# Layer 0's finish: gate in 64-row tiles on half of two banks, x reloaded in 2 KB runs, gate, z and transposes on every fourth token

## The chip, the cores and the metric

The kernel runs on one core of a Trainium2 chip. The number that counts is the device time of one execution in microseconds (us). The profile is one execution taken by the hardware profiler; its times are microseconds from the span's start unless marked ns. PE is TensorE's matmul side, PEld its weight loads, DVE is VectorE, ACT is ScalarE, POOL is GpSimd, SP is the engine that issues the DMAs.

## What is computed

The input x is 256 x 256 positions ("tokens") of 64 channels. Two layers follow each other. Layer 0, which the change touches, is

```
g  = group_norm(x)                      # 32 groups of 2 channels over all tokens
zn = layer_norm(g) * w + b              # over the 64 channels of a token
a  = sigmoid(zn @ w_ag + b_ag) * (zn @ w_ap + b_ap);  b = the same with w_bg, w_bp
p[i,j,c] = sum_k a[i,k,c] * b[j,k,c]    # 64 products of 256 x 256 matrices
x  = x + (layer_norm(p) @ w_z + b_z) * sigmoid(zn @ w_g + b_g)
```

Layer 1 has the same shape, with norms over the whole tensor. Its input is the x of the last line above, group-normalised.

## The kernel before

Rows of x (256 tokens each) are handled in groups of four: 64 groups, NG = 64, GR = 4. Two tokens share a column of the data kept on chip: partitions 0 to 63 hold the channels of an even token, 64 to 127 those of the odd token beside it, so a group is a 128 x 512 tile, four blocks of 128 token pairs. XT_ALL holds zn, transposed in this manner, as a high and a low half in fp16; `half(g, 0)` and `half(g, 1)` are those of group g, each 512 columns in token order. w_hi and w_lo (in EFF) are the two fp16 halves of the weights. The gate's weights stand there as a 128 x 128 matrix with two 64 x 64 blocks on the diagonal (one for the even, one for the odd token) and zeros beside them.

Layer 0 goes through these stages, in time: x is loaded and transposed (L515), normalised, split into halves; then four chunks of channels, each with a projection (L501 with EFF,XT_ALL, in units of eight rows) and an einsum (L501 with AB); the products p go to DRAM (p_scratch). In the projection every second unit is computed in 64-row tiles: two matmuls on partitions 0 to 63 and 64 to 127 with 64 columns each, writing two banks. The other units use 128-row matmuls with 128 columns. Both take x as the loaded operand ("weights" in the profile's sense) and the layer's weights as the streamed one.

Then comes layer 0's finish, the stage of the change, 64 groups in one software pipeline. On TensorE, step k does, in this order:

- 4 transposes of the scaled p of group k (L782), from tile pn into bank 4 or 5;
- the gate of group k (`project_gate`, 12 matmuls of 128 x 128), into bank 0 or 1 in turn, after a wait for the sigmoid of group k-2 (`sg_done`). Groups 0 to 3 (AHEAD = 4) were done before, in banks 0 to 3, in the last chunk;
- z of group k-1: a bias matmul of 512 columns (PS<-BROW,ONES) and 4 fp32 matmuls with pt as loaded operand and w_out streamed (PS<-EFF,WK; the trace shows each as two records), into bank 6 or 7;
- 4 transposes of the new x of group k-3 (L814), from tile xb, into bank 2 or 3.

ACT evicts the transposed p into pt (L993), applies the sigmoid to the gate (L998) and writes the high half of the new x (L1006). DVE scales half of p (L1427), multiplies z by the gate (L1436), writes the low half of the new x (L1450) and takes its statistics (L1442); at steps 3, 6 and 9 it also computes a further quarter of the layer norm's factors (reciprocal L1372 and what follows). POOL scales the other half of p (L1058) and adds the gated z to x (L1067). SP loads p (L415) and x (L421) ahead, x in 16 rows per slot (xb, four slots, two DMAs each), as `x_tok`: for a row of x, partition p takes tokens 2p and 2p+1, 512 bytes in a run. The engines are ordered by semaphores alone; the code's order is the order on each engine.

After the finish comes layer 1: its projection and einsum in four chunks, and its own finish, whose transposes (L767) read a tile at every fourth column, `x1sum[:, g%4, r:BANK:GR]`. The stage that loads x at the start of the kernel already uses `x_runs`, in which partition 32r + p takes eight tokens of row r, 2 KB in a run.

Of the kernel before, what the change touches and what calls it, by code (L numbers as in the profile page):

```python
# [34 lines left out]
CH = 64  # L35
P = 128
# [56 lines left out]
def build(nc, x, mask, w0, w1, bias0, bias1, vecs, consts, norm_consts, spread, ones3, out):  # L93
# [7 lines left out]

    x_tok = x[0].rearrange("r (p q) c -> p r (q c)", q=2)
    x_runs = x[0].rearrange("(g r) (p w) c -> (r p) g (w c)", r=GR, w=2 * GR)
# [6 lines left out]
    with ctx:  # L110
# [82 lines left out]
        ptb = AB[:, 0:2 * CH * BR * 2].rearrange("p (s m n) -> p s m n", s=2, n=2 * BR)  # L193
        xb = AB[:, 2 * CH * BR * 2:4 * CH * BR * 2].rearrange("p (s r m) -> p s r m", s=HS, m=ROW)

# [157 lines left out]
        def mask_tile(eng, n4, u):  # L353
# [3 lines left out]
                                     rows.unsqueeze(2).to_broadcast([P, 2, 2 * CHUNK, PR]), ALU.mult)  # L357

        def reached(eng, semaphore, value):

            if not isinstance(value, int) or value > 0:
                eng.wait_ge(semaphore, value)
# [3 lines left out]
        def _(sp):  # L366
# [22 lines left out]
            for layer in range(2):  # L389
# [29 lines left out]
                def load_rows(row, s):  # L419
                    for h in range(2):  # L420
                        sp.dma_start(xb[:, s, h * HR // 2:(h + 1) * HR // 2, :],  # L421
                                     x_tok[:, ds(row + h * HR // 2, HR // 2), :]).then_inc(xb_in[s], 16)

# [48 lines left out]
                load_rows(0, 0)  # L472
                load_rows(HR, 1)
                load_p(BR, 1)
                load_rows(2 * HR, 2)
                load_rows(3 * HR, 3)

                with sp.Fori(0, NB // 2 - 1) as b2:
                    for s in range(2):
                        for h in range(2):  # L480
                            slot = 2 * s + h
                            row = sp.snap(b2 * (2 * BR) + (slot * HR + HS * HR))
                            p_row = sp.snap(b2 * (2 * BR) + (s * BR + 2 * BR))
                            groups = sp.snap(b2 * (2 * BG) + ((slot + 1) * HG))
                            tiles = sp.snap(b2 * (2 * BG) + ((s + 1) * BG))

                            sp.wait_ge(x1tr_done, groups)
                            load_rows(row, slot)
                            if h == 0:

                                sp.wait_ge(tb_done, tiles)
                                load_p(p_row, s)
# [6 lines left out]
        def _(pe):  # L499
# [116 lines left out]
            for layer in range(2):  # L616

                free = sqp_ready if layer == 0 else st_ready

                def rows_times(bank, g, r, column):  # L620

                    dst = bank[:, r * ROW:(r + 1) * ROW]
                    hi, lo = (half(g, i)[:, r * P:(r + 1) * P] for i in range(2))
                    mm(dst, hi, w_hi[:, ds(column, ROW)], True, False)
                    mm(dst, hi, w_lo[:, ds(column, ROW)], False, False)
                    return mm(dst, lo, w_hi[:, ds(column, ROW)], False, True)

# [40 lines left out]
                def project_gate(g):  # L668
                    if layer == 0:
                        for r in range(GR):  # L670
                            last = rows_times(PS[:, g if g < AHEAD else g % 2, :], g, r, E_G)
                        last.then_inc(g_done, 1)
                    else:
                        bank, hi, lo = PS[:, g % 4, :], w_hi[:, E_G:E_Z], w_lo[:, E_G:E_Z]
                        mm(bank, hi, half(g, 0), True, False)
                        mm(bank, lo, half(g, 0), False, False)
                        mm(bank, hi, half(g, 1), False, True).then_inc(gate1_done, 1)
# [97 lines left out]
                for step in range(NG + 3):  # L775
# [8 lines left out]
                    if AHEAD <= g < NG:  # L784

                        pe.wait_ge(sg_done, g - 1)
                        project_gate(g)
                    g = step - 1
                    if 0 <= g < NG:

                        pe.wait_ge(pt_ready, g + 1)
                        reached(pe, y_done, g - 1)
                        bank = PS[:, 6 + g % 2, :]
                        mm(bank, ONES3[:, :], BROW[:, :].unsqueeze(1).to_broadcast([P, GR, ROW]), True, False)
                        for r in range(GR):
                            last = mm(bank[:, r * P:(r + 1) * P], pt[:, g % 2, r * P:(r + 1) * P], w_out,
                                      False, r == GR - 1)
                        last.then_inc(z_done, 1)
                    g = step - 3
                    if 0 <= g < NG:  # L800

                        pe.wait_ge(xadd_done, g + 1)
                        if g < 2:

                            pe.wait_ge(sg_done, g + 3)
                        if g < NG - 2:

                            reached(pe, x1split_done, g - 1)
                        else:

                            pe.wait_ge(sg_done, NG)
                        for r in range(GR):
                            row = g * GR + r
                            last = nc.tensor.transpose(PS[:, new_x_bank(g), r * P:(r + 1) * P],  # L814
                                                       xb[:, row // HR % HS, row % HR, :], ident)
                        last.then_inc(x1tr_done, 1)
# [13 lines left out]
        def _(act):  # L830
# [54 lines left out]
            for layer in range(2):  # L885
# [99 lines left out]
                def finish_steps(g0, n_steps, lo):  # L985

                    for k in range(n_steps):
                        g = g0 + k
                        if lo[0] <= k < lo[1]:
# [7 lines left out]
                            reached(act, xadd_done, g - 3)  # L997
                            nc.scalar.activation(sg[k % 4], PS[:, k if ahead else k % 2, :], ACT.Sigmoid,  # L998
                                                 scale=T[:, 22:23]).then_inc(sg_done, 1)
                        if lo[2] <= k < lo[3]:  # L1000
                            h = g - 4

                            act.wait_ge(x1tr_done, h + 1)
                            act.wait_ge(bn_done, h + (1 + NG))
                            bank = new_x_bank(h) if isinstance(h, int) else 2 + k % 2
                            nc.scalar.activation(half(h, 0), PS[:, bank, :], ACT.Identity, scale=T[:, 25:26]  # L1006
                                                 ).then_inc(x1t_ready, 1)
# [11 lines left out]
        def _(pool):  # L1019
# [22 lines left out]
            def finish_steps(g0, n_steps, lo):  # L1042
                for k in range(n_steps):
# [16 lines left out]
                    if lo[2] <= k < lo[3]:  # L1060
# [4 lines left out]
                        pool.wait_ge(y_done, h + 1)  # L1065
                        rows = xb[:, slot, u * GR:(u + 1) * GR, :].rearrange("p r m -> p (r m)")
                        nc.gpsimd.tensor_tensor(rows, rows, sg[(k + 1) % 4], ALU.add).then_inc(xadd_done, 1)  # L1067
# [39 lines left out]
        def _(dve):  # L1107
# [14 lines left out]
            def col(i):  # L1122
                return T[:, i:i + 1]
# [191 lines left out]
            for layer in range(2):  # L1315
# [128 lines left out]
                def split(k, g, lo):  # L1444

                    if lo[6] <= k < lo[7]:
                        h = g - 5
                        dve.wait_ge(x1t_ready, h + 1)
                        bank = new_x_bank(h) if isinstance(h, int) else 2 + (k + 1) % 2
                        V.scalar_tensor_tensor(half(h, 1), PS[:, bank, :], col(25), half(h, 0),  # L1450
                                               ALU.mult, ALU.subtract).then_inc(x1split_done, 1)
# [139 lines left out]
```

## Time and profile before

| | |
|---|---|
| median of 3 runs | 1089.46 us (1088.4 to 1090.19) |
| profiled execution | 1086.74 us, its span 1084.9 us |
| granted TensorE clock over the span | 0.964 |
| TensorE matmul busy | 982.9 us, 91% of the span |
| DVE, ACT, POOL busy | 774.3, 677.2, 558.3 us |
| layer 0's finish | from 487.5 to about 659 us |

The span is the time from the first to the last instruction of the program that was profiled. In the trace a matmul's record starts when it enters the array and ends after its modelled latency, so records overlap; the pace of matmuls is read from the distance of their starts, and a merged row "start, length, x12" says where twelve of them began. A busy share of 100% on PE says that no gap was seen between such overlapping records.

### The profile page before, as it was taken

Reading aid. Unit: us, or ns where it says so; the run is one execution under the profiler, and the core shown is the slowest. Engines: PE = TensorE matmul, PEld = TensorE weight load, DVE = VectorE, ACT = ScalarE, POOL = GpSimd, SP = SyncE. Lnnn points to the kernel's source line nnn. Section 1 sums busy time; section 2 is a strip of 40 time slices with the busy share of each in tenths; the row PEclk is TensorE's granted clock in tenths of the full one; section 3 lists DMA queues with packets and bytes.
Section 4 is the critical chain, followed back from the end, with each engine's and each line's share of the span. In section 5 each row is a group of like instructions: output and inputs, shape, how many; then the busy total and the mean of one; then the engine's idle time right before and its main releaser. Section 6 shows DMA issues by size and latency. Waiting matters only on the chain.

```text
span 1084.9 us, 38124 instructions
## 1 busy us (share of the span) xinstructions
PE 982.9 (91%) x15292; PEld 783.0 (72%) x15292; DVE 774.3 (71%) x1278; ACT 677.2 (62%) x1098; POOL 558.3 (51%) x480
## 2 busy tenths in 40 slices
PE   5688888699999999969999995899999999799997
PEld 5533333498888988968999994778878787655554
DVE  6926777876868868678888887655646565567776
ACT  5747666555656666555777674676858676546665
POOL 0002555783470916506777772572918457146664
PEclk9979999799999999989999997899999999889999
DMA  9900000002203021279998930004040220699994
GB/s 342 350 10 1 2 2 2 2 4 78 81 6 153 4 98 61 59 212 255 210 199 185 209 74 1 3 13 147 4 139 22 75 86 11 179 214 272 286 282 156
DMA packets 173205, 121.80 MB, mean 112 GB/s; under 512 B 69764, under 2 KB 152068, under 8 KB 173064
## 3 DMA queue, kind: packets, MB, share of 16 engines
q1 hardware_dynamic: 173064, 119.67, 41.2%
q8 instruction: 119, 1.95, 0.8%
q14 instruction: 22, 0.18, 0.1%
HBM read 69.32 MB, written 50.33 MB: 110 GB/s over the span
## 4 chain that ended last, share of the span: by engine, by line
PE 80%; DVE 7%; DMA 4%; ACT 3%; POOL 2%; issue 2%; SPq 1%; DVEq 0%; POOLq 0%; ACTq 0%
PE PS L501 70%; DMA AB<-x 3%; PE PS L767 3%; PE PS L782 3%; PE PS L814 2%; PE PS L588 2%; POOL XT_ALL L1023 1%; POOL AB L356 1%; PE PS L515 1%; DMA AB<-k_scratch 1%; DVE XT_ALL L1450 1%; ACT XT_ALL L866 1%; ACT WK L903 1%; SPq L370 1%; DVE XT_ALL L1290 0%
## 5 line engine op out<-in xcount | busy, mean ns | idle before, releaser
L501 PE MATMUL PS<-EFF,XT_ALL 64*128 64x64 f16 (+1 forms) x10368 | 344.5, 201 | 11.0 <-POOL XT_ALL L1023 3.4
L501 PEld LDWEIGHTS PS<-EFF,XT_ALL 64*128 64x128 f16 (+1 forms) x10368 | 317.3, 97 | 44.3 <-issue 18.6
L501 PE MATMUL PS<-AB 64*128 64x128 bf16 (+2 forms) x2058 | 233.5, 282 | 12.3 <-POOL AB L1087 6.2
L903 ACT ACTIVATE WK<-PS,T 128x512 f32<-128x512 f32 x256 | 174.5, 685 | 95.5 <-PE PS L501 85.1
L501 PEld LDWEIGHTS PS<-AB 64*128 64x128 bf16 (+2 forms) x2058 | 197.3, 121 | 48.1 <-issue 13.1
L1087 POOL TENSOR_TENSOR AB<-WK,AB 128x512 f32 x128 | 145.1, 1161 | 111.4 <-ACT AB L913 110.6
L356 POOL TENSOR_TENSOR AB<-WK,MS 128x512 f32 x96 | 130.5, 1387 | 104.9 <-DVE WK L1323 104.9
L1023 POOL TENSOR_TENSOR XT_ALL<-AB,XT_ALL 128x512 f16<-128x512 f32 x60 | 71.1, 1189 | 144.0 <-DVE XT_ALL L1290 137.6
L1097 POOL TENSOR_TENSOR WK<-XT_ALL 128x512 f32 (+1 forms) x64 | 81.9, 1282 | 76.3 <-PE PS L767 50.9
L1331 DVE TENSOR_TENSOR WK<-PS,WK 128x512 f32<-128x512 f32 x128 | 85.8, 686 | 33.3 <-ACT WK L903 33.1
L1323 DVE TENSOR_TENSOR WK<-PS,WK 128x512 f32<-128x512 f32 x128 | 86.8, 689 | 29.1 <-ACT WK L903 23.5
L1347 DVE BATCH_NORM_STATS2 REC<-WK 128x512 f32 x64 | 44.4, 694 | 56.8 <-ACT WK L932 56.8
L954 ACT ACTIVATE WK<-PS,T 128x512 f32<-128x512 f32 x64 | 49.4, 777 | 51.4 <-PE PS L501 51.4
L932 ACT ACTIVATE WK<-PS,T 128x512 f32<-128x512 f32 x64 | 44.0, 687 | 51.7 <-PE PS L501 51.7
L501 PE MATMUL PS<-XT_ALL,AB 128*128 128x512 f32 x128 | 74.2, 669 | 0.0
L939 ACT ACTIVATE WK<-PS 128x512 f32<-128x512 f32 x64 | 41.2, 644 | 47.3 <-PE PS L501 45.6
L866 ACT ACTIVATE XT_ALL<-PS,T,CF 128x512 f32<-128x512 f32 x64 | 49.7, 776 | 33.1 <-PE PS L501 32.6
L501 PE MATMUL PS<-AB,EFF 128*128 128x512 f32 x128 | 67.4, 613 | 2.2 <-DMA AB<-k_scratch 2.2
L501 PEld LDWEIGHTS PS<-EFF,WK 128*128 128x128 f32 x512 | 68.1, 194 | 1.8
L1058 POOL TENSOR_TENSOR WK<-AB,S 128x256 f32<-128x256 f32 x64 | 50.5, 789 | 36.2 <-DVE S L1375 35.7
L501 PE MATMUL PS<-EFF,WK 128*128 128x128 f32 x512 | 68.3, 277 | 0.0
L993 ACT ACTIVATE WK<-PS 128x512 f32<-128x512 f32 x64 | 38.2, 597 | 47.4 <-PE PS L782 47.4
(193 smaller groups left out, 1541.4 us busy)
## 6 DMA issues: line engine op xcount, KB each, us to landing
AB<-x SPq DMA_DIRECT2D x64, 512.0 KB, 6.9
p_scratch<-WK SPq DMA_DIRECT2D x32, 512.0 KB, 2.6
k_scratch<-WK SPq DMA_DIRECT2D x64, 256.0 KB, 2.1
AB<-k_scratch SPq DMA_DIRECT2D x32, 512.0 KB, 10.9
out<-AB SPq DMA_DIRECT2D x16, 1024.0 KB, 9.4
AB<-p_scratch SPq DMA_DIRECT2D x29, 512.0 KB, 7.8
AB<-p_scratch SPq DMA_DIRECT2D x2, 640.0 KB, 5.7
AB<-spread SPq DMA_DIRECT2D x1, 832.0 KB
```

The source lines that it names most:

```text
L356: return eng.tensor_tensor(ab[:, :, :, ds(n4 * (4 * PR) + u * PR, PR)], sig[:, u], rows.unsqueeze(2).to_broadcast([P, 2, 2 * CHUNK, PR]), ...
L501: return nc.tensor.matmul(dst, lhsT, rhs, start=start, stop=stop)
L866: nc.scalar.activation(XT[:, n * GR:(n + 1) * GR, :].rearrange("p r n -> p (r n)"), cs_bank(n), ACT.Identity, bias=T[:, 15:16], scale=CF[: ...
L903: nc.scalar.activation(tile, unit(layer, u)[:, :, 0:2 * CHUNK, :], ACT.Sigmoid, scale=T[:, 22:23] if layer == 0 else T[:, 28:29]).then_inc ...
L954: nc.scalar.activation(gate1[:, k % 4], PS[:, k % 4, :], ACT.Sigmoid, bias=T[:, 32:33], scale=T[:, 28:29]).then_inc(gate1_ready, 1)
L1023: nc.gpsimd.tensor_tensor(half(n, 1), zn[:, n % 8], half(n, 0), ALU.subtract).then_inc(lo_done, 1)
L1058: nc.gpsimd.tensor_tensor(dst[:, 1], src[:, 1, :, u * GR:(u + 1) * GR, :], rs.to_broadcast([P, CH // 2, GR, 2]), ALU.mult).then_inc(pn_don ...
L1087: nc.gpsimd.tensor_tensor(ab_rows(ab_lo, n8, u), sig1[:, u], ab_rows(ab_hi, n8, u), ALU.subtract).then_inc(ablo_done, 1)
L1097: nc.gpsimd.tensor_tensor(x1sum[:, k % 4], half(g, 0), half(g, 1), ALU.add).then_inc(x1sum_done, 1)
L1323: V.tensor_tensor(gate, lin, gate, ALU.mult).then_inc(prod_done[0], 1)
L1331: V.tensor_tensor(gate, lin, gate, ALU.mult).then_inc(prod_done[1], 1)
L1347: V.bn_stats(REC[:, ds((q * CHUNK + c) * 6, 6)], st1[:, c % 4]).then_inc(acc_done, 1)
```

## The change

Four things are edited, all in layer 0's finish.

1. Loads of x use `x_runs`: four DMA-contiguous pairs per partition, 2 KB in a run; xb is now indexed by group. The new x of a group therefore comes out of the transposes with column k*128 + n for token pair 4n + k.
2. To match, the gate takes every fourth column of `half(g, i)` as loaded operand, and z every fourth column of pt; ACT's and DVE's writes of the new halves read the bank in the order that brings the columns back into token order (`transposed_bank`, `in_order`).
3. For groups 4 to 63 the gate is computed in 64-row tiles: 24 matmuls of 64 rows and 64 columns in place of 12 of 128 and 128, even tokens into columns 0 to 255 of bank 0, odd tokens into those of bank 1. Groups 0 to 3 keep the 128-row form (with every fourth column).
4. A group's gate now takes parts of both banks, so it waits for the sigmoid of the group just before it (`sg_done` at g, not g - 1), and the sigmoid reads both banks.

```diff
-    x_tok = x[0].rearrange("r (p q) c -> p r (q c)", q=2)
     x_runs = x[0].rearrange("(g r) (p w) c -> (r p) g (w c)", r=GR, w=2 * GR)
...
+        def in_order(tile):
+            return tile.rearrange("p (n k) -> p n k", k=GR)
+        def transposed_bank(bank):
+            return PS[:, bank, :].rearrange("p (k n) -> p n k", k=GR)
...
                 def load_rows(row, s):
                     for h in range(2):
-                        sp.dma_start(xb[:, s, h * HR // 2:(h + 1) * HR // 2, :],
-                                     x_tok[:, ds(row + h * HR // 2, HR // 2), :]).then_inc(xb_in[s], 16)
+                        sp.dma_start(xb[:, s, h * HG // 2:(h + 1) * HG // 2, :],
+                                     x_runs[:, ds(row + h * HG // 2, HG // 2), :]).then_inc(xb_in[s], 16)
...
-                def rows_times(bank, g, r, column):
-                    dst = bank[:, r * ROW:(r + 1) * ROW]
-                    hi, lo = (half(g, i)[:, r * P:(r + 1) * P] for i in range(2))
-                    mm(dst, hi, w_hi[:, ds(column, ROW)], True, False)
-                    mm(dst, hi, w_lo[:, ds(column, ROW)], False, False)
-                    return mm(dst, lo, w_hi[:, ds(column, ROW)], False, True)
+                def split_x(g, k):
+                    hi, lo = (half(g, i)[:, k:BANK:GR] for i in range(2))
+                    return enumerate(((hi, w_hi), (hi, w_lo), (lo, w_hi)))
...
                 def project_gate(g):
-                    if layer == 0:
-                        for r in range(GR):
-                            last = rows_times(PS[:, g if g < AHEAD else g % 2, :], g, r, E_G)
+                    if layer == 0 and g < AHEAD:
+                        for k in range(GR):
+                            for i, (x, w) in split_x(g, k):
+                                last = mm(PS[:, g, k * ROW:(k + 1) * ROW], x, w[:, E_G:E_G + ROW], i == 0, i == 2)
+                        last.then_inc(g_done, 1)
+                    elif layer == 0:
+                        for k in range(GR):
+                            for i, (x, w) in split_x(g, k):
+                                for q in range(2):
+                                    rows = slice(q * CH, (q + 1) * CH)
+                                    last = mm(PS[:, q, k * CH:(k + 1) * CH], x[rows, :],
+                                              w[rows, E_G + q * CH:E_G + (q + 1) * CH], i == 0, i == 2)
                         last.then_inc(g_done, 1)
...
-                        pe.wait_ge(sg_done, g - 1)
+                        pe.wait_ge(sg_done, g)
                         project_gate(g)
...
-                            last = mm(bank[:, r * P:(r + 1) * P], pt[:, g % 2, r * P:(r + 1) * P], w_out,
-                                      False, r == GR - 1)
+                            last = mm(bank[:, k * P:(k + 1) * P], pt[:, g % 2, k:BANK:GR], w_out,
+                                      False, k == GR - 1)
...
-                            nc.scalar.activation(sg[k % 4], PS[:, k if ahead else k % 2, :], ACT.Sigmoid,
-                                                 scale=T[:, 22:23]).then_inc(sg_done, 1)
+                            if ahead:
+                                nc.scalar.activation(sg[k % 4], PS[:, k, :], ACT.Sigmoid,
+                                                     scale=T[:, 22:23]).then_inc(sg_done, 1)
+                            else:
+                                nc.scalar.activation(sg[k % 4].rearrange("p (k q c) -> p k q c", k=GR, q=2),
+                                                     PS[:, 0:2, 0:GR * CH].rearrange("p q (k c) -> p k q c", k=GR),
+                                                     ACT.Sigmoid, scale=T[:, 22:23]).then_inc(sg_done, 1)
...
-                            nc.scalar.activation(half(h, 0), PS[:, bank, :], ACT.Identity, scale=T[:, 25:26]
+                            nc.scalar.activation(in_order(half(h, 0)), transposed_bank(bank), ACT.Identity, scale=T[:, 25:26]
...
-                        V.scalar_tensor_tensor(half(h, 1), PS[:, bank, :], col(25), half(h, 0),
+                        V.scalar_tensor_tensor(in_order(half(h, 1)), transposed_bank(bank), col(25), in_order(half(h, 0)),
```

On TensorE, in the steady part of the finish, one step reads before the change as follows (L814 and L782 are the two sets of transposes, the rows with EFF,XT_ALL the gate, BROW,ONES the bias and EFF,WK z; "x11" counts instructions alike):

```order
L814 MATMUL PS<-CF,AB 128x128 [waits x1split_done,xadd_done]
L814 MATMUL PS<-CF,AB 128x128 x3
L782 MATMUL PS<-CF,WK 128x128 [waits pt_ready,pn_done_p,pn_done]
L782 MATMUL PS<-CF,WK 128x128 x3
L501 MATMUL PS<-EFF,XT_ALL 128x128 [waits sg_done]
L501 MATMUL PS<-EFF,XT_ALL 128x128 x11
L501 MATMUL PS<-BROW,ONES 128x512 [waits y_done,pt_ready]
L501 MATMUL PS<-EFF,WK 128x128 x4
```

The same step in the changed kernel, whose line numbers are 7 to 13 higher:

```order
L826 MATMUL PS<-CF,AB 128x128 [waits x1split_done,xadd_done]
L826 MATMUL PS<-CF,AB 128x128 x3
L795 MATMUL PS<-CF,WK 128x128 [waits pt_ready,pn_done_p,pn_done]
L795 MATMUL PS<-CF,WK 128x128 x3
L508 MATMUL PS<-EFF,XT_ALL 128x64 [waits sg_done]
L508 MATMUL PS<-EFF,XT_ALL 128x64 x23
L508 MATMUL PS<-BROW,ONES 128x512 [waits y_done,pt_ready]
L508 MATMUL PS<-EFF,WK 128x128 x4
```

Nothing changes its place: only the gate's twelve matmuls have become twenty-four with 64 columns each, between transposes and a bias matmul that both use all 128 rows.

Where the finish begins, on TensorE too, the first step with a gate of its own (group 4) reads before

```order
L814 MATMUL PS<-CF,AB 128x128 [waits sg_done,xadd_done]
L814 MATMUL PS<-CF,AB 128x128 x3
L782 MATMUL PS<-CF,WK 128x128 [waits pt_ready,pn_done_p,pn_done]
L501 MATMUL PS<-EFF,XT_ALL 128x128 [waits sg_done]
L501 MATMUL PS<-EFF,XT_ALL 128x128 x11
```

and in the changed kernel

```order
L826 MATMUL PS<-CF,AB 128x128 [waits sg_done,xadd_done]
L826 MATMUL PS<-CF,AB 128x128 x3
L795 MATMUL PS<-CF,WK 128x128 [waits pt_ready,pn_done_p,pn_done]
L508 MATMUL PS<-EFF,XT_ALL 128x64 [waits sg_done]
L508 MATMUL PS<-EFF,XT_ALL 128x64 x23
```

The steps ahead of it have no gate, so 60 of the 64 groups change form.

## Rows read from the trace of the kernel before

**Rows 1.** The page: busy time by engine.

```profile
PE 982.9 (91%) x15292; PEld 783.0 (72%) x15292; DVE 774.3 (71%) x1278; ACT 677.2 (62%) x1098; POOL 558.3 (51%) x480
```

**Rows 2.** Chain that ended last, layer 0's finish: start, length, what.

```profile
511.88 0.30 DVE S L1375
...
514.57 0.66 PE PS L782 x4
...
655.24 0.44 PE PS L782 x4
```

**Rows 3.** Timeline of PE, one step of the finish: start, length of merged records.

```profile
599.86 0.83 PE L501 MATMUL PS<-EFF,XT_ALL 128*128 128x128 f16 x12
600.53 0.38 PE L501 MATMUL PS<-BROW,ONES 128*128 128x512 bf16 x1
600.75 1.05 PE L501 MATMUL PS<-EFF,WK 128*128 128x128 f32 x8
601.64 0.60 PE L814 MATMUL PS<-CF,AB 128*128 128x128 f32 x4
602.08 0.60 PE L782 MATMUL PS<-CF,WK 128*128 128x128 f32 x4
602.51 0.50 PE L501 MATMUL PS<-EFF,XT_ALL 128*128 128x128 f16 x6
```

**Rows 4.** Waits between 515 and 655 us: us in total, times, longest.

```profile
ACT WK L993 <- PE PS L782: 37.2, 53, 0.8
...
DVE MS L1436 <- PE PS L501: 8.4, 26, 0.3
```

**Rows 5.** Timeline of PE in layer 1's projection: one 64-row unit and what follows.

```profile
700.18 0.86 PE L501 MATMUL PS<-EFF,XT_ALL 64*128 64x64 f16 x48
700.88 0.38 PE L501 MATMUL PS<-BIASR,ONES 64*128 64x512 bf16 x2
```

**Rows 6.** Window in layer 0's projection: PE, PEld, DVE, ACT, POOL busy (count), clock, DMA.

```profile
220.13:238.15 18.02, 18.02 (x582) 16.78 (x576) 13.46 (x20) 10.93 (x16) 15.11 (x13) 1.00 0.02 5
```

**Rows 7.** Timeline of PE in layer 1's finish, around the transposes of every fourth column.

```profile
1042.40 0.64 PE L767 MATMUL PS<-CF,WK 128*128 128x128 f32 x4
1042.87 1.02 PE L501 MATMUL PS<-AB,EFF 128*128 128x512 f32 x2
...
1042.62 0.41 PE L767 MATMUL PS<-CF,WK 128*128 128x128 f32 x2
```

**Rows 8.** Weight loads by line: duration in ns, min/median/max.

```profile
L767 PEld LDWEIGHTS PS<-CF,WK x256: 196/210/221, 957.0 to 1079.1; 128*128 128x128 f32 x128
...
L814 PEld LDWEIGHTS PS<-CF,AB x256: 138/141/144, 494.7 to 661.7; 128*128 128x128 f32 x128
```

**Rows 9.** Groups by form, 515 to 655 us: weight loads of z and gate (busy us, mean ns).

```profile
L501 PEld LDWEIGHTS PS<-EFF,WK 128*128 128x128 f32 x424 | 55.6, 192 | 1.4
...
L501 PEld LDWEIGHTS PS<-EFF,XT_ALL 128*128 128x128 f16 x636 | 39.9, 98 | 0.6
```

**Rows 10.** Timeline of weight loads after the 128-row unit.

```profile
702.63 0.10 PEld L501 LDWEIGHTS PS<-BIASR,ONES 64*128 64x128 bf16 x2
702.64 0.10 PEld L501 LDWEIGHTS PS<-EFF,XT_ALL 64*128 64x128 f16 x2
```

**Rows 11.** Timelines of ACT and DVE beside the step of Rows 3.

```profile
602.72 0.60 ACT L993 ACTIVATE WK<-PS 128x512 f32<-128x512 f32 x1 [0.71 <-PE PS L782]
603.39 0.69 ACT L998 ACTIVATE MS<-PS,T 128x512 f32<-128x512 f32 x1
...
604.49 0.69 DVE L1436 TENSOR_TENSOR MS<-PS,MS 128x512 f32<-128x512 f32 x1 [0.32 <-PE PS L501]
```

**Rows 12.** Windows in the finish, columns as in Rows 6, DMA share next to last.

```profile
600.00:610.00 10.00, 10.00 (x113) 9.86 (x111) 8.77 (x16) 7.45 (x12) 8.11 (x8) 1.00 1.30 238
...
640.00:650.00 10.00, 10.00 (x112) 9.86 (x109) 8.77 (x16) 7.26 (x12) 7.82 (x8) 1.00 0.00 0
```

**Rows 13.** Groups by form: ACT reading a bank in transposed order.

```profile
L835 ACT ACTIVATE XT_ALL<-PS 128x512 f32 x48 | 24.8, 603 | 8.2 <-PE PS L515 8.2
```

More of the change, by code:

```diff
@@ L193, in build @@
         ptb = AB[:, 0:2 * CH * BR * 2].rearrange("p (s m n) -> p s m n", s=2, n=2 * BR)
-        xb = AB[:, 2 * CH * BR * 2:4 * CH * BR * 2].rearrange("p (s r m) -> p s r m", s=HS, m=ROW)
+        xb = AB[:, 2 * CH * BR * 2:4 * CH * BR * 2].rearrange("p (s g n) -> p s g n", s=HS, n=BANK)
         kt = AB[:, 0:PS1 * PR1 * P].rearrange("p (s n) -> p s n", s=PS1)
@@ L472, in _ @@
                 load_rows(0, 0)
-                load_rows(HR, 1)
+                load_rows(HG, 1)
                 load_p(BR, 1)
-                load_rows(2 * HR, 2)
-                load_rows(3 * HR, 3)
+                load_rows(2 * HG, 2)
+                load_rows(3 * HG, 3)
                 with sp.Fori(0, NB // 2 - 1) as b2:
@@ L481, in _ @@
                             slot = 2 * s + h
-                            row = sp.snap(b2 * (2 * BR) + (slot * HR + HS * HR))
+                            row = sp.snap(b2 * (2 * BG) + (slot * HG + HS * HG))
                             p_row = sp.snap(b2 * (2 * BR) + (s * BR + 2 * BR))
@@ L794, in _ @@
                         mm(bank, ONES3[:, :], BROW[:, :].unsqueeze(1).to_broadcast([P, GR, ROW]), True, False)
-                        for r in range(GR):
-                            last = mm(bank[:, r * P:(r + 1) * P], pt[:, g % 2, r * P:(r + 1) * P], w_out,
-                                      False, r == GR - 1)
+                        for k in range(GR):
+                            last = mm(bank[:, k * P:(k + 1) * P], pt[:, g % 2, k:BANK:GR], w_out,
+                                      False, k == GR - 1)
                         last.then_inc(z_done, 1)
@@ L811, in _ @@
                             pe.wait_ge(sg_done, NG)
[L812 to L815, printed above, removed]
+                        for k in range(GR):
+                            last = nc.tensor.transpose(PS[:, new_x_bank(g), k * P:(k + 1) * P],
+                                                       xb[:, g // HG % HS, g % HG, k * P:(k + 1) * P], ident)
                         last.then_inc(x1tr_done, 1)
@@ L1065, in finish_steps @@
                         pool.wait_ge(y_done, h + 1)
-                        rows = xb[:, slot, u * GR:(u + 1) * GR, :].rearrange("p r m -> p (r m)")
+                        rows = xb[:, slot, u, :]
                         nc.gpsimd.tensor_tensor(rows, rows, sg[(k + 1) % 4], ALU.add).then_inc(xadd_done, 1)
```

## The prediction

> **What bounds the kernel now.** I read the busy shares first. TensorE is the busiest engine over the whole span [rows 1], but a share over the span mixes stages, so I went to the only stage that is edited, layer 0's finish. In the chain of waits its first part is paced by DVE: until 512 us DVE's extra factor work (L1375) stands on the chain. From the transposes at 514.57 us to those at 655.24 us the chain is TensorE alone [rows 2]. One step there, from the first gate matmul to the next group's first, is 602.51 - 599.86 = 2.65 us, and its parts leave no gap: gate 0.67, bias 0.22, z 0.89, transposes of x 0.44, transposes of p 0.43 [rows 3]. (655.24 - 514.57) / 2.65 = 53 periods, so 54 groups take their gate in this regime. The waits of this stretch say the same from the other side: ACT, POOL and DVE wait for PE, directly or through one another, and no wait of PE is among them [rows 4]. So a nanosecond taken from or added to TensorE's step counts 54 times. It counts little in steps 4 to 9, where DVE sets the pace, and nowhere else.
>
> **The sum, part by part.** Each figure is for one step.
>
> Gate in 64-row tiles. Twelve full matmuls take 0.67 us, 56 ns each [rows 3]. In 64-row form a pair of matmuls runs side by side: 48 of them from 700.18 to 700.88, 29 ns a pair [rows 5]. Twelve pairs are 0.35 us. But the array has to go from 128 rows to 64 and back, between neighbours that use all rows. What that costs stands in layer 0's projection, where 64-row and 128-row units alternate: the window holds 576 weight loads, 72 per pair of units, so eight pairs in 18.02 us, 2.25 us each [rows 6]. Matmuls at full pace would be 24 x 56 ns and 24 x 29 ns, together 2.04. The other 0.21 us is one switch in and one out. Every step of the changed stage has exactly such a pair of switches. Gate after: 0.35 + 0.21 = 0.56 us, against 0.67. Saved: 0.11 us.
>
> z with every fourth column of pt. The loaded operand is now strided fp32. The trace has such loads once, in layer 1's finish: a strided load lasts 196 to 221 ns, a contiguous one of the same kind of transpose 138 to 144 [rows 8]. What matters is the pace. The four strided transposes run from 1042.40 to 1042.87, 0.47 us against the 0.44 of contiguous ones [rows 3, 7]; the last two of the four are 0.25 us from the next matmul, 125 ns each, while the first two still profit from the long matmul ahead of them. z's eight records run at 111 ns now and follow a 512-column bias, the same situation. Two at the early pace (0.22) and six at 125 ns give 0.97 us against 0.89: 0.08 us lost, 0.07 if I use 123 ns, which the rounding allows. The bound below is nothing: z's contiguous load already lasts 192 ns [rows 9], nearly the 196 of a strided transpose, so perhaps its 111 ns stays. The bound above is all eight at 125 ns, 0.11. I take 0.075, since the strided load of rows 7 would be the same instruction apart from the transpose.
>
> Gate with every fourth column of the fp16 halves. No row shows a strided fp16 load. Contiguous ones last 98 ns [rows 9] and can follow each other 10 to 20 ns apart [rows 10]. The fp32 rows tell what striding takes: a transpose's contiguous load (141) is 51 ns shorter than z's contiguous one (192), and with a stride it becomes 197 or more. That looks like a fixed part of about 86 ns and a streaming part of 55 that doubles. With the same fixed part a contiguous fp16 load streams for some 12 to 15 ns, a strided one for 24 to 30. That is the pace of a pair, 29 ns, so it is just hidden; I take 30 ns a pair (+0.012) and the first load behind the switch, which nothing covers, 13 ns longer (+0.013). Bounds: nothing below; above, a pair at the 125 ns of the strided fp32 load, 12 x 0.096 = +1.15 us.
>
> By the Trainium skill ("SBUF — State Buffer", Specifications (TRN2), the line on cachelines) consecutive reads keep full rate as long as at least two fall in one 16-byte line: every fourth fp16 does, every fourth fp32 does not. The trace agrees for fp32, 125 against 111 ns. By that rule the gate's loads would stay at 12 to 15 ns and the sum below would be 1.4 us lower; no run here shows it yet.
>
> The wait for the sigmoid of the group just before. Gate of the next group starts 2.65 us after this one's at 602.51; the sigmoid it would now wait for runs from 603.39 to 604.08 [rows 11]. It is over 1.1 us before it is wanted. It starts behind ACT's eviction at 602.72, not behind the gate, so a faster gate doesn't pull the margin in. Nothing. If that cover were gone, everything behind it on TensorE (z, both sets of transposes) would be late by the difference, and with them ACT, which waits for L782, and DVE.
>
> x in 2 KB runs. The load is hidden: the step takes the same time where the DMA engines are at 1.30 and at 0.00 of their share, 113 and 112 matmuls in 10 us [rows 12]. The same number and size of DMAs are issued on SP's queue in the same places. Nothing in either direction; if transfers became slower, POOL's addition would be the one to wait.
>
> Evictions in transposed order. ACT reads so already, 603 ns [rows 13] against 0.60 us for its plain copy L993; it is idle 0.71 us per step [rows 11]. DVE is idle 0.32 us per step before L1436 [rows 11]. A few ns on either are covered.
>
> Sum: -0.106 + 0.075 + 0.013 + 0.012 = -0.006 us a step, times 54 = -0.3 us. The profiled execution took 1086.74 us (span 1084.9) and would take 1086.4. The runs shown have their median 2.7 us above it, 1089.46; taking the difference over gives 1089.1, and I write 1089.0. A gain of 0.11 and losses of about 0.1 meet here, so the answer is no change that can be told. A measurement of this kernel tells about 0.2%, 2.2 us or 0.04 us a step, from no change.
>
> **Rivals.**
>
> *z's strided loads cost nothing* (their 192 ns were paid already), and half loads neither. Then the step is 2.65 - 0.10 = 2.55 us; DVE's busy time, 8.77 of 10 us or 2.32 a step [rows 12], still fits. -0.092 x 54 = -5.0 us: 1084.5. For it speaks z's long contiguous load; against it the pace of 125 ns that a strided load has as soon as it has no cover. Chance 0.20.
>
> *The gate's strided fp16 loads set the pace* (the other side: slower). The place is the twelve pairs; the price is 12 ns a step for each ns that a pair takes beyond 30. It decides from 34 ns on (+0.04 a step, 2.2 us). If the loads of the two tiles have to follow one another, or lose their fast form in part, a pair takes some 56 ns: 0.31 more, +17 us, 1106. At the full fp32 pace it is +1.13, 1150. For it: this load is unlike any in the trace, and a pair has only 29 ns in which two loads must be in. Against it: the doubling estimate lands at 24 to 30, and the two tiles' loads start side by side in the trace [rows 10]. Chance 0.25, most of it between 34 and 60 ns.
>
> *The sum holds within 2 us*: 0.47, of which 0.04 falls just past each bound. *The single-buffered gate waits*, or another new wait shows, price a few tenths of a us a step, some 3 to 15 us: 0.04, against it the 1.1 us of margin. *The x loads matter after all* (a shorter start of the stage, 1 to 5 us faster): 0.04, against it that the first steps wait for DVE, not for a DMA.
>
> **How the numbers follow.** Faster by over 0.2%: 0.20 + 0.04 + 0.02 of the sum's lower edge = 0.26. Slower: 0.25 + 0.04 + 0.02 = 0.31. Within: 0.43. The range has to keep most of the first rival and the near part of the second: 1084.0 to 1097.0 leaves out about 0.05 below and 0.14 above. The likeliest case alone is 1086.8 to 1091.4.
>
> **What the next profile would show.** A steady step within 0.04 us of 2.65. In it the gate's pairs 29 to 31 ns apart, the bias matmul some 0.12 us after the last gate matmul and the first gate matmul some 0.2 us after the last transpose; z's records growing from 111 to about 122 ns; weight loads of z near 210 ns and of the gate near 110. No wait of PE for L998's successor. A steady step of 2.55 with z at 111 ns proves the first rival; pairs wider than 34 ns the second. The prediction is wrong in its frame if PE waits at all between 515 and 655 us, or if the time moves outside the finish.

## The result, and the profile after

The changed kernel takes 1138.52 us (median of 4 runs, 1136.91 to 1141.15) against 1089.18 for the kernel before in the same comparison: 1.0455 times the time, 95% interval 1.0432 to 1.0477. That is 49 us slower, far above the range of the prediction. The profiled execution has a span of 1135.1 us against 1084.9.

The page after, busy time by engine and z's weight loads, a group of L508 (the matmul line, L501 before; columns as in the page: busy us, mean ns of one, idle before):

```profile
PE 1034.2 (91%) x16012; PEld 825.9 (73%) x16012; DVE 776.6 (68%) x1278; ACT 678.4 (60%) x1098; POOL 558.6 (49%) x480
...
L508 PEld LDWEIGHTS PS<-EFF,WK 128*128 128x128 f32 x512 | 124.6, 326 | 0.3
```

TensorE is busy for 51 us more, while DVE, ACT and POOL do the same work in the same time. z's weight loads, 192 ns before [rows 9], last 326 ns on average. The transposes of p mark the stage; their first and last start, before (L782) and after (L795), are

```profile
L782 PE MATMUL PS<-CF,WK x256: 272/273/445, 487.5 to 655.4; 128*128 128x128 f32 x128
```

```profile
L795 PE MATMUL PS<-CF,WK x256: 272/273/444, 489.2 to 704.0; 128*128 128x128 f32 x128
```

The stage grew from 167.9 to 214.8 us, 46.9 of the 50.2 by which the span grew. Of the rest, 1.7 us lie ahead of it, in code whose order and operands are the same but for the first four gates; in the experiments below, whose code up to there is that of one of the two kernels, that start moves between 487.8 and 494.3 us too, so nothing can be made of 1.7 us. The other 1.6 us lie behind the last transposes; no run separates them.

One steady step of the changed kernel on PE (timeline: start, length of merged records), to be laid beside [rows 3]:

```profile
603.14 0.60 PE L795 MATMUL PS<-CF,WK 128*128 128x128 f32 x4
603.67 0.59 PE L508 MATMUL PS<-EFF,XT_ALL 64*128 64x64 f16 x24
604.20 0.39 PE L508 MATMUL PS<-BROW,ONES 128*128 128x512 bf16 x1
604.42 1.91 PE L508 MATMUL PS<-EFF,WK 128*128 128x128 f32 x8
606.17 0.60 PE L826 MATMUL PS<-CF,AB 128*128 128x128 f32 x4
606.61 0.27 PE L795 MATMUL PS<-CF,WK 128*128 128x128 f32 x1
```

From transposes to transposes it is 606.61 - 603.14 = 3.47 us, where it was 2.65. z takes 606.17 - 604.42 = 1.75 us against 0.89, so from the second record on, where the bias no longer covers the load, one starts every 233 ns instead of every 111. The gate runs from 603.67 to 604.20, 0.53 us against 0.67, but the transposes ahead of it last 0.53 up to its start instead of 0.43: the first switch of form stands there. And TensorE, not DVE, now sets the pace from the first gates on. The chain of waits in the part where DVE's factor work stood on it before [rows 2]:

```profile
502.80 0.44 PE PS L795 x4
503.23 2.59 PE PS L508 x33
505.82 0.44 PE PS L826 x4
506.26 0.44 PE PS L795 x4
```

The steps with a gate of their own all run at 3.47 us: the 59 distances from one group's transposes to the next, from group 4 on, are 3.46 or 3.47 us. Before, 57 of them were 2.65 to 2.71 us and two early ones, with DVE's work in them, 4.12 and 3.68. The other engines only wait for longer. Here are the waits between 515 and 700 us (us in total, times, longest), to be laid beside those between 515 and 655 us before [rows 4]; ACT now waits 1.6 us each time for the transposes, where it was 0.7:

```profile
ACT WK L1005 <- PE PS L795: 83.0, 53, 1.7
...
DVE MS L1453 <- PE PS L508: 29.2, 26, 1.1
```

### The profile page after: what moved, and what is told of

It reads as the page before. It is cut to its first block, busy times and chain, and to the rows that moved or that the text cites. A ratio compares the mean times of both kernels' runs of the same rounds, so it can differ in the third digit from the quotient of the medians.

```text
span 1135.1 us, 39561 instructions
## 1 busy us (share of the span) xinstructions
PE 1034.2 (91%) x16012; PEld 825.9 (73%) x16012; DVE 776.6 (68%) x1278; ACT 678.4 (60%) x1098; POOL 558.6 (49%) x480
## 4 chain that ended last, share of the span: by engine, by line
PE 82%; DVE 5%; DMA 4%; ACT 3%; POOL 2%; issue 2%; SPq 1%; DVEq 0%; POOLq 0%; ACTq 0%
PE PS L508 72%; DMA AB<-x 3%; PE PS L795 3%; PE PS L780 3%; PE PS L826 2%; PE PS L595 2%; POOL AB L355 1%; POOL XT_ALL L1040 1%; DMA AB<-k_scratch 1%; PE PS L522 1%; ACT XT_ALL L878 1%; SPq L377 1%; ACT WK L915 1%; DVE XT_ALL L1307 0%; DVE WK L1340 0%
## 5 line engine op out<-in xcount | busy, mean ns | idle before, releaser
L508 PEld LDWEIGHTS PS<-EFF,XT_ALL 64*128 64x128 f16 (+1 forms) x11088 | 301.5, 99 | 53.3 <-issue 28.4
L508 PE MATMUL PS<-EFF,XT_ALL 64*128 64x64 f16 (+1 forms) x11088 | 330.2, 200 | 10.8 <-POOL XT_ALL L1040 3.2
L508 PE MATMUL PS<-AB 64*128 64x128 bf16 (+2 forms) x2058 | 233.5, 282 | 13.3 <-POOL AB L1104 6.2
L508 PEld LDWEIGHTS PS<-AB 64*128 64x128 bf16 (+2 forms) x2058 | 197.5, 122 | 49.1 <-issue 13.1
L508 PEld LDWEIGHTS PS<-EFF,WK 128*128 128x128 f32 x512 | 124.6, 326 | 0.3
L508 PE MATMUL PS<-EFF,WK 128*128 128x128 f32 x512 | 122.5, 383 | 0.0
L508 PE MATMUL PS<-XT_ALL,AB 128*128 128x512 f32 x128 | 74.0, 668 | 0.0
L508 PE MATMUL PS<-AB,EFF 128*128 128x512 f32 x128 | 67.9, 616 | 2.5 <-DMA AB<-k_scratch 2.5
```

Of the source, the lines that this page charges most:

```text
L508: return nc.tensor.matmul(dst, lhsT, rhs, start=start, stop=stop)
```

## The experiments

**Undo the strided load of z alone.** ACT evicts the transposed p with every fourth column side by side, and z loads contiguous columns; everything else is the changed kernel.

```diff
-nc.scalar.activation(pt[:, k % 2], PS[:, 4 + k % 2, :], ACT.Copy)
+nc.scalar.activation(pt[:, k % 2].rearrange("p (k n) -> p k n", k=GR),
+                     PS[:, 4 + k % 2, :].rearrange("p (n k) -> p k n", k=GR), ACT.Copy)
...
-    pt[:, g % 2, k:BANK:GR], w_out,
+    pt[:, g % 2, k * P:(k + 1) * P], w_out,
```

> The changed kernel, except that ACT writes the evicted p into pt with every fourth column side by side, so that z loads contiguous columns again; the computation is whole. Theory 1 (all of the loss is z's strided fp32 load): z's eight records are back at 111 ns, 0.89 us in all, and the step is the 3.47 us seen less 0.86, 2.61 us, 0.04 us under before; 54 steps give about 2.3 us less than before, some 1087 us. Theory 2 (z's loads are slow because they follow the 64-row tiles and a switch of form, whatever their stride): z stays near 233 ns a record, the step at 3.4 to 3.5 us, the time near 1138 us.

Measured: 1087.89 us against 1090.21, ratio 0.9978 (0.9963 to 0.9993). All of the loss is gone and a small gain stands. Its step on PE:

```profile
601.25 0.39 PE L508 MATMUL PS<-BROW,ONES 128*128 128x512 bf16 x1
601.47 1.05 PE L508 MATMUL PS<-EFF,WK 128*128 128x128 f32 x8
602.36 0.60 PE L826 MATMUL PS<-CF,AB 128*128 128x128 f32 x4
...
603.33 0.58 PE L508 MATMUL PS<-EFF,XT_ALL 64*128 64x64 f16 x24
603.85 0.39 PE L508 MATMUL PS<-BROW,ONES 128*128 128x512 bf16 x1
```

z is 0.89 us again, directly behind the same 64-row gate; the step, 603.85 - 601.25, is 2.60. Theory 2 is out.

**Do the strided load of z alone**, in the kernel before. z is then that of other tokens.

```diff
-    mm(bank[:, r * P:(r + 1) * P], pt[:, g % 2, r * P:(r + 1) * P], w_out,
+    mm(bank[:, r * P:(r + 1) * P], pt[:, g % 2, r:BANK:GR], w_out,
```

> The kernel before with one edit: z loads every fourth column of pt (so z belongs to other tokens than it should; everything else is as before, the 128-row gate too). Theory 1: z's records go from 111 to 233 ns, the step from 2.65 to 3.51 us, and with DVE's own pace hidden in all steps the time rises by about 50 us to some 1139 us. Theory 2: no 64-row tiles, no loss: 1089 us, step 2.65.

Measured: 1143.29 us, ratio 1.0486 (1.0465 to 1.0507). Without any 64-row tile in the stage, z is as slow:

```profile
600.52 1.92 PE L501 MATMUL PS<-EFF,WK 128*128 128x128 f32 x8
602.28 0.60 PE L814 MATMUL PS<-CF,AB 128*128 128x128 f32 x4
```

1.76 us for z, the step 603.82 - 600.31 = 3.51 us in the same timeline. Together the two runs show the cause from both sides.

**The size of the step.** The same edit with every second and with every third column (`pt[:, g % 2, r // 2 * 2 * P + r % 2:(r // 2 + 1) * 2 * P:2]` and `pt[:, g % 2, r:r + 3 * P:3]`), z again of other tokens.

> The kernel before with z loading every second column of one half of pt (z then belongs to other tokens). If what costs is that no two of the loaded words share 16 bytes (theory 1a), two still do here: records stay at 111 to 123 ns, the weight load at about 197 ns, step 2.65 to 2.75, time 1087 to 1094 us. If any stride costs as much (theory 1b), records at 233 ns, step 3.51, time about 1138 us.

> The kernel before with z loading every third column of pt (z then belongs to other tokens). Words 12 bytes apart: of four, two still share 16 bytes. If only words without a partner in their 16 bytes cost more, the records lie between the 118 ns of every second column and the 233 of every fourth, near 170; step about 3.1 us, time about 1115 us. If the cost is a threshold on the step itself, 118 or 233 ns.

Measured, one run each: 1089.62 us (before: 1090.21) and 1113.62 us (before: 1090.73). The timelines of z, every second column and every third:

```profile
602.53 1.10 PE L501 MATMUL PS<-EFF,WK 128*128 128x128 f32 x8
603.47 0.60 PE L814 MATMUL PS<-CF,AB 128*128 128x128 f32 x4
```

```profile
602.16 1.50 PE L501 MATMUL PS<-EFF,WK 128*128 128x128 f32 x8
603.49 0.60 PE L814 MATMUL PS<-CF,AB 128*128 128x128 f32 x4
```

z takes 0.94 and 1.33 us. Past the first record, which the bias still covers, that is 118 and about 175 ns a record, beside 111 contiguous and 233 at every fourth. The loads of one window, 530 to 640 us, by form (busy us, mean ns of one), for every second, third and fourth column in turn:

```profile
L501 PEld LDWEIGHTS PS<-EFF,WK 128*128 128x128 f32 x327 | 44.9, 197 | 0.8
```

```profile
L501 PEld LDWEIGHTS PS<-EFF,WK 128*128 128x128 f32 x286 | 54.3, 260 | 0.0
```

```profile
L501 PEld LDWEIGHTS PS<-EFF,WK 128*128 128x128 f32 x253 | 61.5, 326 | 0.0
```

128 fp32 columns at these steps lie in 64, 96 and 128 pieces of 16 bytes. 118, 175 and 233 ns divided by them are 1.84, 1.82 and 1.82 ns a piece. So the price is not that of a stride as such; it grows in proportion to the pieces touched. That it is the pieces, and not the step itself, isn't shown: up to a step of 16 bytes the two grow together, 58 to 59 ns for each column of step, and no run has a longer one. My estimate, by 111 ns divided by 1.82, is that up to about 61 pieces cost nothing.

**Why the price in the prediction was another.** It was taken from transposes. These two kernels put strided loads on the transposes of p in this very stage, at every fourth and every second column of pn (values of p are mixed up; z is contiguous): `pn[:, g % 2].rearrange("p r m -> p (r m)")[:, r:BANK:GR]`, and the same with a step of 2.

> The kernel before with the four transposes of p loading every fourth column of pn (channels and rows of p are mixed up, so z is of other values). This puts the strided transpose, which the prediction priced z by, into z's own stage. If the low price belongs to the transpose itself, loads near 210 ns, records at about 122, the step 0.04 to 0.06 us longer: 2.70 us, 1091 to 1093 us. If it was the place in layer 1's finish that made it cheap, records near 233 ns, the step 0.4 us longer, about 1115 us.

> As tr_step4, but the transposes of p load every second column, 8 bytes apart (values of p are mixed up). For z and for the fp16 gate the price went by how many 16-byte pieces of a partition the columns lie in (64, 96, 128 of them: 118, 175, 233 ns). If the transposes follow a law of the same kind at half the price, half as many pieces as in tr_step4 leave them at the 109 ns of contiguous columns, step 2.65 us, 1089 to 1090 us. If what they lose is only the reading of two neighbours at once, any step costs the same: loads near 210 ns, 118 to 122 ns each, step 2.69 to 2.70 us as in tr_step4.

Measured, one run each: 1091.13 us (before: 1090.73) and 1093.82 us (before: 1090.29). What tells them apart is the step in the profile, 2.70 and 2.69 us, since a single run's time is not exact to 2 us. With every fourth column the four transposes take 603.08 - 602.60 = 0.48 us, 120 to 123 ns each:

```profile
602.60 0.65 PE L782 MATMUL PS<-CF,WK 128*128 128x128 f32 x4
603.08 0.83 PE L501 MATMUL PS<-EFF,XT_ALL 128*128 128x128 f16 x12
```

The mean load of both, 530 to 640 us, every fourth and every second column:

```profile
L782 PEld LDWEIGHTS PS<-CF,WK 128*128 128x128 f32 x162 | 22.9, 209 | 0.0
```

```profile
L782 PEld LDWEIGHTS PS<-CF,WK 128*128 128x128 f32 x162 | 22.7, 206 | 0.0
```

A transpose pays 11 to 14 ns: 120 ns with every second column and 120 to 123 with every fourth, for 109 contiguous. So it pays hardly more for 128 pieces than for 64. The first half of the expectation (a law at half the price) falls; the second holds. The cheap strided load is the transpose's own: it is as cheap here as in layer 1's finish.

**The gate in 64-row tiles alone.** The kernel before with `project_gate`, wait and sigmoid of the change, but token order kept, so nothing is strided:

```diff
+for r in range(GR):
+    hi, lo = (half(g, i)[:, r * P:(r + 1) * P] for i in range(2))
+    for i, (x, w) in enumerate(((hi, w_hi), (hi, w_lo), (lo, w_hi))):
+        for q in range(2):
+            rows = slice(q * CH, (q + 1) * CH)
+            last = mm(PS[:, q, r * CH:(r + 1) * CH], x[rows, :],
+                      w[rows, E_G + q * CH:E_G + (q + 1) * CH], i == 0, i == 2)
```

> The kernel before with the gate in 64-row tiles on half of two banks, the sigmoid over both and the wait for the group just before, and nothing strided; the computation is whole. By the prediction's price (0.35 us of pairs and 0.21 us of switches for 0.67): step 2.54 us, 5.7 us less than before, 1083.5 us. By what the changed kernel showed from the last transpose to the first z record (0.954 us against 0.995, part of it the strided fp16 loads at the start): step 2.57 to 2.61 us, 2 to 4.5 us less, 1085 to 1087 us. Theory 2 (64-row tiles make the loads behind them slow): a step above 2.65, slower than before.

Measured: 1084.57 us against 1090.21, ratio 0.9953 (0.9935 to 0.9970), faster than both kernels. Its chain of waits:

```profile
541.24 0.44 PE PS L791 x4
541.67 1.67 PE PS L501 x33
543.34 0.44 PE PS L823 x4
543.78 0.44 PE PS L791 x4
```

The step is 543.78 - 541.24 = 2.54 us, 0.11 under the 2.65 before. That is what pairs at 29 ns and two switches were priced at. Measured against pt_reordered's 2.61, every fourth fp16 column costs 0.06 us a step. Theory 2 is out here too.

**A longer stride for the fp16 loads.** As gate_alone, with every eighth column over both halves of a group, 16 bytes apart (the gate mixes halves and tokens):

```diff
-hi, lo = (half(g, i)[:, r * P:(r + 1) * P] for i in range(2))
+both = halves[:, ds(g * (2 * BANK), 2 * BANK)]
+hi, lo = (both[:, 2 * r + i:2 * BANK:8] for i in range(2))
```

> As gate_alone, but the gate loads every eighth fp16 column over the two halves of a group, 16 bytes apart (the gate is then of mixed halves and tokens; z is contiguous). gate_alone's pairs (4-byte steps apart none: contiguous) run at 29 ns and those with every fourth fp16, 8 bytes apart, at about 33. If fp16 loads double once more when no two columns share 16 bytes, as z's did between 8 and 16 bytes, a pair takes some 60 ns and the step about 2.92 us, time about 1106 us. If fp16 loads don't mind, the step is 2.61 us, time about 1088.

Measured, one run: 1104.59 us (before: 1090.73), step 2.94. The gate, from its first matmul to the bias:

```profile
602.25 0.92 PE L501 MATMUL PS<-EFF,XT_ALL 64*128 64x64 f16 x24
603.10 0.39 PE L501 MATMUL PS<-BROW,ONES 128*128 128x512 bf16 x1
```

0.85 us for twelve pairs and the switch behind them, 60 ns a pair in the middle. The gate's loads of a window, contiguous (gate_alone), every fourth (pt_reordered) and every eighth column:

```profile
L501 PEld LDWEIGHTS PS<-EFF,XT_ALL 64*128 64x128 f16 x1032 | 17.5, 95 | 7.2 <-issue 7.2
```

```profile
L508 PEld LDWEIGHTS PS<-EFF,XT_ALL 64*128 64x128 f16 x1020 | 20.5, 115 | 7.2 <-issue 7.2
```

```profile
L501 PEld LDWEIGHTS PS<-EFF,XT_ALL 64*128 64x128 f16 x888 | 30.2, 162 | 6.2 <-issue 6.2
```

Pairs at 29, 33 and 60 ns. The 16-byte pieces are 16, 64 and 128. The fp16 load's price fits them too, at roughly a quarter of z's, 33 for 64 and 60 for 128; here as well the step in bytes (2, 8 and 16) grows along with them.

**The other parts.** The kernel before with only the reload of x in 2 KB runs (x, z and gate of different tokens are then added), and the changed kernel with its gate back in 128-row form and the old wait:

```diff
-sp.dma_start(xb[:, s, h * HR // 2:(h + 1) * HR // 2, :], x_tok[:, ds(row + h * HR // 2, HR // 2), :])
+sp.dma_start(xbg[:, s, h * HG // 2:(h + 1) * HG // 2, :], x_runs[:, ds(row + h * HG // 2, HG // 2), :])
```

```diff
-                    if layer == 0 and g < AHEAD:
+                    if layer == 0:
...
-                        pe.wait_ge(sg_done, g)
+                        pe.wait_ge(sg_done, g - 1)
```

> The kernel before with only the reload of x in 2 KB runs (gate and z stay in token order, so x, z and gate of different tokens are added). The prediction: nothing, 1089 to 1091 us, step 2.65 us, while the DMA share in the stage falls from about 0.95 to about 0.7. Rival: the start of the stage or its tail gains 1 to 5 us.

> The changed kernel with the gate in its old 128-row form, in one bank in turn, with the old wait; x in 2 KB runs, every fourth column for gate and z; the computation is whole. If the strided fp16 load is hidden behind a 56 ns matmul and z costs 0.86 us as before, the step is 2.65 + 0.86 = 3.51 us, as in z_step4, and the time is z_step4's, about 1142 us. If the strided fp16 load costs the 128-row gate as well, a step above 3.55 us and 1145 us or more.

Measured: 1089.32 us, ratio 0.9990 (0.9977 to 1.0003), and 1144.20 us, ratio 1.0496 (1.0472 to 1.0520). The window 520 to 630 us before and with the 2 KB runs (PE, PEld, DVE, ACT, POOL busy, clock, DMA share, GB/s):

```profile
520.00:630.00 110.00, 110.00 (x1208) 108.44 (x1207) 97.36 (x167) 77.10 (x125) 83.98 (x83) 1.00 0.98 202
```

```profile
520.00:630.00 110.00, 110.00 (x1203) 108.45 (x1201) 97.00 (x167) 77.74 (x126) 84.44 (x84) 1.00 0.86 197
```

The DMA engines' share falls from 0.98 to 0.86 (at 202 and 197 GB/s; over the whole kernel the bytes are the same), less than expected, and the step is 2.65 us in both. With the 128-row gate the step is z_step4's 3.51 us; its strided fp16 loads last 113 ns instead of 98 and hide behind matmuls 56 ns apart. So the 64-row gate saves 0.05 us of a step in the changed kernel.

**Half of the switches.** Built on gate_alone: gates of two groups one behind the other in every second step, the second in columns 256 to 511 of the two banks; the first one's sigmoid waits for both.

```diff
-                        pe.wait_ge(sg_done, g)
-                        project_gate(g)
+                        if g % 2 == 0:
+                            pe.wait_ge(sg_done, g)
+                            project_gate(g)
+                            project_gate(g + 1)
...
-                            act.wait_ge(g_done, g + 1)
+                            act.wait_ge(g_done, g + 1 if ahead or k % 2 else g + 2)
```

> As gate_alone (nothing strided; the computation is whole), but TensorE computes the gates of two groups behind each other in every second step, the second group in columns 256 to 511 of the two banks, and the first group's sigmoid waits for both. Half of the switches between 128-row and 64-row form are gone. If the switches are what gate_alone still pays (0.21 us a pair of them), two steps take 2 x 2.543 - 0.21 us, 2.44 us each, and the time falls by another 5.5 us to some 1079 us. Rival: DVE, busy 2.33 us a step, or ACT's later sigmoid paces the uneven steps and the time stays at gate_alone's 1084.5.

Measured: 1085.06 us, ratio 0.9951 (0.9935 to 0.9968), the same as gate_alone. The rival holds:

```profile
540.93 0.66 PE PS L792 x4
541.59 2.02 PE PS L501 x57
543.61 0.44 PE PS L826 x4
544.04 0.44 PE PS L792 x4
544.48 1.11 PE PS L501 x9
545.59 0.44 PE PS L826 x4
546.02 0.00 issue
546.03 0.66 PE PS L792 x4
```

Two steps are 546.03 - 540.93 = 5.10 us. That is gate_alone's 2 x 2.54, though one pair of switches fewer was expected to save 0.21. The short step's work would end 0.2 us earlier, but the transposes at its end (0.66 instead of 0.44) wait for DVE's half of p, as the waits between 530 and 640 us name it:

```profile
PEld PS L792 <- DVE WK L1444: 5.2, 22, 0.2
```

DVE's four operations stand back to back in the short step. In the long one DVE is idle before it multiplies z:

```profile
594.65 0.69 DVE L1453 TENSOR_TENSOR MS<-PS,MS 128x512 f32<-128x512 f32 x1 [0.48 <-PE PS L501]
```

So it is the unequal halves that DVE doesn't follow. It is busy for 101.69 of the 110 us from 530 to 640, an estimated 2.36 us a step of 2.55; whether equal steps under 2.54 us are possible no run here shows.

## Why the prediction was wrong

**What bounds the stage** was right: TensorE's own work, no wait, a nanosecond counted once for every step. It was to count 54 times; with z so much longer, DVE's work in the early steps was covered too, and those steps lost as well, though less each. The sign for a wrong frame, time moving outside the finish, is not quite absent either: 3.3 of the 50.2 us lie there, unexplained.

**The gate in 64-row tiles** was right. 0.56 us for 0.67 was worked out from layer 0's projection; gate_alone measured a step 0.107 us shorter and a time 5.6 us shorter. That the price came out within 1 ns is partly luck: its terms go back to rows rounded to 10 ns. By the Trainium skill ("TensorEngine Tiling (Array Packing)", Key Properties) a change of tiling mode drains the array; the trace agrees, with about 0.1 us for each of the two switches between transposes, gate and bias.

**z with every fourth column of pt** is the step that failed: "I take 0.075, since the strided load of rows 7 would be the same instruction apart from the transpose." It measured 0.86 us, eleven times as much, far over the upper bound that the text gave it, 0.11. That bound was again the pace of the transposes, so the range could not hold the result. z_step4 shows the price alone, pt_reordered shows that nothing else was lost, and tr_step4 and tr_step2 show that the row chosen behaves otherwise: a strided transpose takes 120 to 123 ns at both steps, a strided fp32 matmul load 118, 175 and 233 as the step grows. Why the two differ stays open. A warning stood in the rows. Contiguous, the two loads last 141 and 192 ns [rows 8, 9]; a matmul load and a transpose load are not alike without a stride, and nothing said that they are with one. The text even used a fixed part of 86 ns and a streaming part that doubles for the fp16 loads, and left z out; on z's 192 ns that rule gives 298, near the 308 to 330 measured here for single loads, and a streaming part of over 200 ns.

Nor is it so that the trace has strided fp32 loads once. Layer 0's einsum loads every second fp32 column (`b[:, h::2]`) for ordinary matmuls. Over the whole kernel before, with six other loads among them:

```profile
L501 PEld LDWEIGHTS PS<-AB 128*128 128x128 f32 x518 | 101.1, 196 | 14.1 <-POOL AB L356 3.6 <-issue 0.5
```

These were the nearer rows, and at their step z_step2 has the same load, 197 ns. About a step of 4 they say nothing, and with the 192 ns of contiguous columns beside them they would have misled just as well.

**Every fourth fp16 column** was of the right kind and too cheap: 0.025 us a step priced, 0.06 measured. The first two pairs behind the switch, whose loads nothing covers, start 55 ns apart in pt_reordered and 39 in gate_alone, and later ones 33 ns, not 30. The rival that named this load as the danger looked at the wrong one of the two; its sign came true through z.

By the Trainium skill ("SBUF — State Buffer", Specifications (TRN2)) a read needs at least two hits in each 16-byte line to keep its rate. The runs bear this out for matmul loads, nearly: with two columns in a line 118 ns for 111 (fp32) and 33 for 29 (fp16), with one 233 and 60. For transposes it doesn't show. The prediction had the rule beside the z load and read the row against it, 125 for 111 ns, as its confirmation; the row was of the wrong instruction.

**The wait for the sigmoid, the 2 KB runs and the evictions** cost nothing, as said. Between 530 and 640 us gate_alone shows no wait of PE; x_runs_alone is at 0.9990. pt_reordered, with all evictions reordered, shows none either, and the 0.06 us by which its step is longer lie in the gate: 601.25 - 600.73 = 0.52 us from its first matmul to the bias, against 605.65 - 605.19 = 0.46.

**The sum**: expected -0.106 + 0.075 + 0.025, measured -0.107 + 0.86 + 0.06, 0.81 us a step; the two profiles give 0.816. Times the 59 distances with a gate it is 48.1 us. From that go the 2.7 us by which DVE had made the early ones longer before, and 1.4 us come on in the four distances ahead of them, where z is strided too: 46.8 us, the stage's 46.9.

One slip in the chances changes nothing of this: the sum's 0.47 is said to fall past each bound with 0.04, but what follows takes 0.02 on either side.

## What to carry to other kernels

Price a load by the same instruction at the same stride, or treat it as unknown and let the range say so: four matmuls with strided fp32 loads in place of contiguous ones cost 0.86 us in a 2.65 us step. Where a layout must be permuted, let an evicting engine with idle time do it on the way out of PSUM (ACT, 0.7 us idle a step, did it for nothing in pt_reordered) and keep loaded operands contiguous; at a step of two fp32 columns z lost only 0.04 us a step. And of a change in several parts, the part that pays may need none of the others: the 64-row gate in token order gives 5.6 us by itself. Next in line there is DVE, busy for 101.03 of 110 us in gate_alone, an estimated 2.34 of its 2.54 us a step.

## What the runs showed of the hardware

Fp32 matmuls with 128 loaded columns start 118, 175 and 233 ns apart where the columns touch 64, 96 and 128 pieces of 16 bytes, 1.82 to 1.84 ns a piece; a step over 16 bytes, which would tell pieces from step, wasn't run. Fp16 pairs start 33 and 60 ns apart for 64 and 128 pieces, about a quarter of that. Transposed fp32 loads run at 120 ns for 64 pieces and 120 to 123 for 128, and at 109 contiguous; why they don't go by pieces is open. The first contiguous load behind a strided one lasts longer too: in z_step4 the first of L814's four has 267 ns and the others 140, 172 on average over the window against 141 [rows 8].
